# A four-layer kernel on one core: both mixtures norm turned rows inside their body and store per tile, and the decay attention norms in its projections and works in 64-token blocks

## The chip, the cores and the metric

The kernel runs on one core of one Trainium2 chip. The metric is the device time of one execution in microseconds (us); less is better. A core has TensorE (PE, with its weight loads shown apart as PEld), VectorE (DVE), ScalarE (ACT), GpSimd (POOL), and SyncE (SP), which here only issues DMAs. Engines run their own programs and wait for each other by semaphores. Everything is f32, so each matmul shows as two passes in the trace.

## The reference, cut to what matters

The input is 4 sequences of 1024 tokens with 128 features. A layer norm stands before each layer, and each layer adds to x:

```python
x = x + attn_a(_layernorm(x), ...)      # delta attention, 8 heads: untouched here
x = x + ffn(_layernorm(x), ...)         # first mixture, "f1"
x = x + attn_b(_layernorm(x), ...)      # decay attention
x = x + ffn(_layernorm(x), ...)         # second mixture, "f2", same weights

# ffn (mixture of 15 experts, 3 used per token, and a shared one)
shared = relu(xt @ sW1 + sb1) @ sW2 + sb2
probs = softmax(xt @ router_W + router_b)
top_p, top_i = top_k(probs, 3)          # cw: those three, zero elsewhere
h = relu(einsum('nd,edh->neh', xt, eW1) + eb1)
routed = einsum('ned,ne->nd', einsum('neh,ehd->ned', h, eW2) + eb2, cw)

# attn_b, per head of 64: a state that decays per feature
state = (1.0 - wt)[..., None] * state + kt[..., None] * vt[..., None, :]
out = einsum('bhd,bhde->bhe', rt, state)
```

## The kernel before

The 4096 tokens lie turned (features on partitions) in `g.xT`, their normed copy in `g.xn`; a tile is 512 tokens, NT = 8.

`build` calls the stages one after another: `delta_attention`, `normed_mixture` "f1", `decay_attention`, `normed_mixture` "f2", `store_rows`. Each is a block of its own with one hand-written program per engine; the order of lines in such a program is the order on that engine, and blocks are parted by a barrier.

`normed_mixture` has two parts. In the lead all eight tiles are normed on turned data (`centre`, `variance` and `replicate` on PE, `take` and `root` on ACT, `invert` and `norm` on DVE), with the router of tile 0 between them. In the body PE goes over tiles n and experts e: `hidden(n, e + 2)` makes a hidden tile into bank `ph`, ACT takes its relu into `hr`, DVE scales it by its gate into `hs`, and PE adds its product to `py`. Tile n's body also makes the router of tile n+1: `r_lt` and `r_tr` on PE, `r_sub`, `r_top`, `r_cwt` on DVE, `r_exp` on ACT. The gates go by SP to DRAM (`gates_d`) and come back spread over all partitions (`gates`, in four groups, double-buffered):

```python
for n in range(NT):
    sp.wait_ge(ct_ev, n + 1)
    sp.dma_start(gates_d[n % 2], cwt[n % 2][0:E_N, :]).then_inc(gates_out, 16)
```

`decay_attention` calls `layernorm`, a block of its own, then projects each tile (five products: z in two steps, k, r, v). `near(l, b)` makes, for level l and sequence b, the 32x32 blocks of a triangular product for levels 0 to 5, which DVE keeps by mask in `Pc`; `merge(l, b)` on DVE then doubles the span of the decays; levels 6 and 7 are `far`, kept by ACT in `P`, where ACT also lays `Pc` down (`spread`). `steps()` gives the order: levels 0 and 1 of a sequence stand behind the tiles that complete it. A scan over chunks ends the stage. `store_rows` turns the result back and stores it in four DMAs.

Of the kernel before, what the change touches and what calls it, by code (L numbers as in the profile page):

```python
# [42 lines left out]
def constants():  # L43
# [14 lines left out]
    s, t = a[:, None] % 32, np.arange(32)[None, :]  # L58
    bm = [(s == t).astype(np.float32)]
    for l in range(5):  # L60
        h = 1 << l
        bm.append(((s // (2 * h) == t // (2 * h)) & (s // h < t // h)).astype(np.float32))
# [19 lines left out]


def store_rows(nc, g):

    with ExitStack() as ctx:  # L86
        new_sem = semaphores(nc, ctx)
        xo = ctx.enter_context(nc.sbuf_tensor("xout", [128, NTOK // 128, D], F32))
        ps = [ctx.enter_context(nc.psum_tensor(f"st{i}", [128, TILE], F32)) for i in range(4)]
        turned, kept, stored = (new_sem(n) for n in ("st_turned", "st_kept", "st_stored"))  # L90
        block = ctx.enter_context(nc.Block())
        dst = g.dram["out"].rearrange("b t d -> (b t) d").rearrange("(j p) d -> p j d", p=128)

        @block.tensor
        def _(pe):
            for i in range(NT):
                if i >= 4:
                    pe.wait_ge(kept, i - 3)
                for a in range(4):
                    o = TILE * (i % 2) + 128 * a  # L100
                    last = nc.tensor.transpose(ps[i % 4][:, 128 * a:128 * a + 128], g.xT[:, i // 2, o:o + 128], g.ident[:, :])  # L101
                last.then_inc(turned, 1)

        @block.scalar
        def _(act):
            for i in range(NT):
                act.wait_ge(turned, i + 1)
                nc.scalar.activation(xo[:, 4 * i:4 * i + 4, :], ps[i % 4][:, :].rearrange("p (a d) -> p a d", a=4), ACT.Copy).then_inc(kept, 1)  # L108

        @block.sync  # L110
        def _(sp):
            for q in range(4):
                sp.wait_ge(kept, 2 * q + 2)
                sp.dma_start(dst[:, 8 * q:8 * q + 8, :], xo[:, 8 * q:8 * q + 8, :]).then_inc(stored, 16)
            sp.wait_ge(stored, 64)


def layernorm(nc, g, tag, src, affine=None, fetch=None, fetched=None):

    QUARTER = TILE // 4  # L120
    EPS = 1e-5
    root_scale, root_bias = (1.0, EPS) if affine is None else (1.0 + EPS, EPS * EPS)
    with ExitStack() as ctx:
        new_sem = semaphores(nc, ctx)
        sb = lambda n, s: ctx.enter_context(nc.sbuf_tensor(tag + n, s, F32))
        pb = lambda n: [ctx.enter_context(nc.psum_tensor(f"{tag}{n}{i}", [128, TILE], F32)) for i in range(2)]
        cen, var, rep = pb("cen"), pb("var"), pb("rep")
        xc = sb("xc", [128, 4, TILE])
        sq = sb("sq", [128, 2, TILE])
        rs = sb("rs", [128, 4, QUARTER])  # L130
        eps = sb("eps", [128, 1])
        centred, squared, copied, varied, rooted, inverted, spread, scaled, normed, eps_ready = (
            new_sem(tag + n) for n in ("centred", "squared", "copied", "varied", "rooted", "inverted", "spread", "scaled", "normed", "eps_ready"))
        block = ctx.enter_context(nc.Block())

        if fetch is not None:
            @block.sync
            def _(sp):
                fetch(sp)

        @block.tensor
        def _(pe):
            def centre(i):
                if i >= 2:
                    pe.wait_ge(copied, i - 1)
                nc.tensor.matmul(cen[i % 2][:, :], g.centre[:, :], src(i), start=True, stop=True).then_inc(centred, 1)

            def variance(i):
                pe.wait_ge(squared, i + 1)
                if i >= 2:  # L150
                    pe.wait_ge(rooted, i - 1)
                for q in range(4):
                    last = nc.tensor.matmul(var[i % 2][32 * q:32 * q + 32, 0:QUARTER], g.mean[:, 0:32], sq[:, i % 2, QUARTER * q:QUARTER * (q + 1)], start=True, stop=True)
                last.then_inc(varied, 1)

            def replicate(i):
                pe.wait_ge(inverted, i + 1)
                if i >= 2:
                    pe.wait_ge(scaled, i - 1)
                for q in range(4):  # L160
                    last = nc.tensor.matmul(rep[i % 2][:, QUARTER * q:QUARTER * (q + 1)], g.pick[:, q, :], rs[:, i % 4, :], start=True, stop=True)
                last.then_inc(spread, 1)
            centre(0)
# [1210 lines left out]
def normed_mixture(nc, g, tag):  # L1374
# [5 lines left out]
    with ExitStack() as ctx:  # L1380
# [62 lines left out]
        def _(pe):  # L1443
# [52 lines left out]
            for i in range(NT + 1):  # L1496
# [6 lines left out]
                if i == 2:  # L1503
                    r_lt(0)
# [528 lines left out]
```

## Time and profile before

| | us |
|---|---|
| three runs | 3269.03, 3266.42, 3254.58 (median 3266.42) |
| profiled execution: its own time | 3265.66 |
| its span in the trace | 3263.9 |
| PE busy | 3048.2 (93%) |
| DVE busy | 2505.7 (77%) |
| ACT busy | 2268.4 (70%) |
| POOL busy | 1947.9 (60%) |

The span is what the trace shows from first to last instruction. Shares are averages over stages with different limits, so what a stage waits for is read in that stage. A row of the timeline gives start, duration, engine, line, operation, output and inputs, shape and count, and in brackets how long the engine sat idle before it and what ended that; a count joins neighbouring instructions of one line.

### The profile page before, as it was taken

How to read it: one execution, taken by the hardware profiler on the slowest of the kernel's cores; microseconds unless marked ns; L12 is line 12 of the kernel's file. 1: busy time of each engine (PE TensorE's matmuls, PEld its weight loads, DVE VectorE, ACT ScalarE, POOL GpSimd, SP SyncE). 2: the span in 40 equal slices, each digit the busy share in tenths (PEclk: the TensorE clock that was granted, in tenths of full speed). 3: DMA queues.
4: the chain of work that ended last, by engine and by line, in shares of the span. 5: the costliest groups of instructions: out<-in, count | busy, mean ns of one | idle time of the engine just before them, and what ended most of it. 6: DMA issues, size and time to landing. Idle time of an engine off the chain costs nothing. (4 is left out here: it accounts for less than half of the span.)

```text
span 3263.9 us, 86845 instructions
## 1 busy us (share of the span) xinstructions
PE 3048.2 (93%) x29020; PEld 2370.3 (73%) x29020; DVE 2505.7 (77%) x5782; ACT 2268.4 (70%) x6848; POOL 1947.9 (60%) x3091
## 2 busy tenths in 40 slices
PE   5569999999999999999999999999998999848998
PEld 3448888888888888888888888888774444545444
DVE  5669999999999999999999999999654443664443
ACT  4768888888888888888888888888543333323333
POOL 1588888888888888888888888888710000000000
PEclk8779999999999999999999999999998999959999
DMA  4456776767777767777677767767432322002323
GB/s 100 122 146 169 190 187 170 178 170 179 182 185 178 173 177 178 174 184 182 176 176 175 179 172 187 183 168 177 122 95 84 137 106 103 5 4 76 146 98 123
DMA packets 587924, 482.94 MB, mean 148 GB/s; under 512 B 464492, under 2 KB 504076, under 8 KB 581340
## 3 DMA queue, kind: packets, MB, share of 16 engines
q1 hardware_dynamic: 587484, 477.39, 55.1%
q8 instruction: 237, 3.88, 0.5%
q14 instruction: 203, 1.66, 0.2%
HBM read 285.39 MB, written 191.86 MB: 146 GB/s over the span
## 5 line engine op out<-in xcount | busy, mean ns | idle before, releaser
L1058 DVE SCALAR_TENSOR_TENSOR conv_k<-PP,tk,conv_k 128x256 f32<-128x256 f32 x1536 | 722.6, 479 | 61.0 <-ACT conv_k L893 33.5
L831 POOL TENSOR_TENSOR X<-X,tmp 96x31 f32<-96x31 f32 (+15 forms) x992 | 534.5, 539 | 77.8
L1058 DVE SCALAR_TENSOR_TENSOR conv_v<-PP,tv,conv_v 128x256 f32<-128x256 f32 x1152 | 539.0, 477 | 45.0 <-ACT conv_v L893 35.4
L828 POOL TENSOR_TENSOR tmp<-At,X 96x31 f32<-96x31 f32 (+15 forms) x992 | 486.3, 490 | 63.2 <-DMA At<-n_d 5.0
L1227 PE MATMUL PP<-xn,wk 128*128 128x268 f32 x1024 | 342.2, 418 | 35.9 <-DVE conv_k L1058 27.9
L814 POOL TENSOR_TENSOR rk<-ss,half 96x8 f32<-96x8 f32 x128 | 209.1, 1633 | 175.1 <-DVE ss L1026 175.1
L796 POOL TENSOR_TENSOR Sg<-S,gend 128x512 f32<-128x512 f32 x256 | 266.0, 1039 | 62.0 <-DVE S L1017 62.0
L865 ACT ACTIVATE recA<-TG,es 96x128 f32<-96x128 f32 x1024 | 285.1, 369 | 5.3 <-DVE es L1051 5.3
L893 ACT ACTIVATE conv_k<-PP,tk 128x256 f32<-128x256 f32 x512 | 245.4, 481 | 54.9 <-PE PP L1227 47.6
L1191 PE MATMUL RB<-rhs,Yf 96*96 96x128 f32 x2048 | 269.0, 274 | 14.6 <-DVE rhs L1006 14.5
L857 ACT ACTIVATE recA<-TG 128x128 f32<-128x128 f32 x1024 | 265.5, 272 | 24.6 <-PE TG L1278 24.6
L883 ACT ACTIVATE ws<-RB 96x512 f32<-96x512 f32 x256 | 151.7, 592 | 184.0 <-PE RB L1191 181.1
L1181 PE MATMUL RA<-S,kqgB 128*96 128x128 f32 x2048 | 276.2, 278 | 1.0 <-DVE S L1017 1.0
L1201 PE MATMUL RA<-ws,recB 96*128 96x128 f32 x2048 | 271.6, 275 | 0.2 <-ACT ws L883 0.2
L1191 PEld LDWEIGHTS RB<-rhs,Yf 96*96 96x96 f32 x2048 | 242.2, 163 | 37.0 <-DVE rhs L1006 24.6
L1201 PEld LDWEIGHTS RA<-ws,recB 96*128 96x128 f32 x2048 | 259.9, 192 | 8.1 <-ACT ws L883 0.8
L1290 PE MATMUL TG<-kq 128*96 128x128 f32 x1888 | 245.2, 273 | 1.2 <-ACT recA L865 1.0
L1181 PEld LDWEIGHTS RA<-S,kqgB 128*96 128x96 f32 x2048 | 233.4, 163 | 13.0 <-DVE S L1017 4.4
L781 POOL TENSOR_TENSOR kqgA<-kq,gdec 128x768 f32<-128x768 f32 x128 | 203.2, 1587 | 38.4 <-ACT kq L934 31.6
L1290 PEld LDWEIGHTS TG<-kq 128*96 128x96 f32 x1888 | 219.0, 163 | 2.2 <-ACT recA L865 2.2
L1227 PE MATMUL PP<-xn,wv 128*128 128x268 f32 x768 | 218.5, 391 | 1.2 <-DVE conv_k L1058 1.2
L1227 PEld LDWEIGHTS PP<-xn,wk 128*128 128x128 f32 x1024 | 161.5, 197 | 67.2 <-issue 34.2
(280 smaller groups left out, 6751.2 us busy)
## 6 DMA issues: line engine op xcount, KB each, us to landing
kqg_d<-kqgA SPq DMA_DIRECT2D x128, 512.0 KB, 6.3
kqgB<-kqg_d SPq DMA_DIRECT2D x128, 512.0 KB, 4.4
rec_d<-recA SPq DMA_DIRECT2D x128, 480.0 KB, 3.4
recB<-rec_d SPq DMA_DIRECT2D x128, 480.0 KB, 5.8
f1gates<-f1gates_d SPq DMA_DIRECT2D x24, 1024.0 KB, 6.8
f2gates<-f2gates_d SPq DMA_DIRECT2D x24, 1024.0 KB, 6.8
gdec<-gdec_d SPq DMA_DIRECT2D x128, 128.0 KB, 5.6
apk_d<-apkA SPq DMA_DIRECT2D x128, 128.0 KB, 3.3
```

The source lines that it names most:

```text
L796: nc.gpsimd.tensor_tensor(Sg[:, :, :], S[cc][:, :, :], d.broadcast_to([128, B, 128]), ALU.mult).then_inc(sg_ev[cc], 1)
L828: nc.gpsimd.tensor_tensor(t, At[q % 2][:, j, j + 1:].unsqueeze(2).broadcast_to(sh), X[q % 2][:, j, 0:cols].unsqueeze(1).broadcast_to(sh), ...
L831: nc.gpsimd.tensor_tensor(x, x, t, ALU.subtract).then_inc(sub_ev, 1)
L857: last = nc.scalar.activation(recA[N % 2][:, u * 128:(u + 1) * 128], TG[:, u, :], ACT.Square, accum_out=ksum[:, u:u + 1])
L865: last = nc.scalar.activation(recA[N % 2][0:R, u * 128:(u + 1) * 128], TG[0:R, u, :], ACT.Copy, scale=es[:, u, TC - 1:TC])
L893: nc.scalar.activation(acc, src[:, :, 0:SPAN], ACT.Copy, scale=w).then_inc(tap0_ev[i], 1)
L1058: return nc.vector.scalar_tensor_tensor(acc, src[:, :, j:j + SPAN], w[:, j:j + 1], acc, ALU.mult, ALU.add)
L1181: last = mm(RA[0:R, b, :], kqgB[N % 2][:, b * NCC + cc, 0:R], S[cc][:, b, :], start=True, stop=True)
L1191: last = mm(RB[0:R, b, :], Yf[N % 2][:, b * NCC + cc, :], rhs[:, b, :], start=True, stop=True)
L1201: last = mm(RA[:, b, :], recB[N % 2][:, u * 128:(u + 1) * 128], ws[cc][:, b, :], start=True, stop=True)
L1227: mm(out, w, x, start=True, stop=True).then_inc(tile_mm[i], 1)
L1290: last = mm(gram_bank(N, hf)[0:R, u % HU, :], kq[N % 2][:, u, 0:R], kq[N % 2][:, u, :], start=True, stop=True)
```

## The change

In both mixtures the norm goes into the body. PE turns a tile back to rows (`rows_of`), DVE centres it (`centre`), ACT squares it with a sum per token (`square`), GpSimd raises variance to -1/2, DVE scales (`norm`), PE turns it again (`hat`), ACT keeps it in `g.xn` (`keep_xn`). Tiles 0 and 1 pass ahead of the body; tile n+2 passes inside tile n. The router's logits come as rows from one set of four matmuls (`r_lg`), and DVE adds the bias. `ph` has three banks. The second mixture stores by tile: `store_turn` on PE, `keep_out` on ACT, `out_rows` on SP; `store_rows` and `layernorm` are gone. In the decay attention the same norm stands in the projections, two tiles ahead, with one bank each for the two turns; the block width W is 64, levels 0 to 6 are near, only 7 is far, and `P` is cleared in eight pieces.

```diff
 @block.sync                                  # normed_mixture
+        def out_rows(sp, n):
+            sp.wait_ge(st_ev, n + 1)
+            dst = d["out"].rearrange("b t d -> (b t) d")[TILE * n:TILE * (n + 1), :].rearrange("(a p) d -> p a d", p=128)
+            sp.dma_start(dst, xo[:, n % 2, :, :]).then_inc(stored[n % 2], 16)
...
                     sp.dma_start(gates[n % 2][:, a:b, :], gates_d[n % 2, a:b].partition_broadcast(128)).then_inc(gates_in[n % 2][k], 16)
+                if last and n:
+                    out_rows(sp, n - 1)
...
 @block.tensor
+            rows_of(0)
+            rows_of(1)
+            hat(0)
+            r_lg(0)
+            hat(1)
...
+                    if e == 1:
+                        rows_of(n + 2)
+                    if e == 11:
+                        hat(n + 2)
                     if n + 1 < NT:
                         if e == 0:
-                            r_lt(n + 1)
-                        if e == 2:
-                            r_tr(n + 1)
+                            r_lg(n + 1)
                         if e == 7:
                             r_ct(n + 1)
+                    if last and n and e == 14:
+                        store_turn(n - 1)
+            if last:
+                store_turn(NT - 1)
...
 @block.scalar
+            def keep_out(n):
+                act.wait_ge(st_mm, n + 1)
+                if n >= 2:
+                    act.wait_ge(stored[n % 2], 16 * (n // 2))
+                nc.scalar.activation(xo[:, n % 2, :, :], turn_bank(0), ACT.Copy).then_inc(st_ev, 1)
...
+                    if e == 6:
+                        square(n + 2)
+                    if e == 13:
+                        keep_xn(n + 2)
+                    if last and n and e == 15:
+                        keep_out(n - 1)
...
 @block.gpsimd
+                nc.gpsimd.tensor_tensor(rs[:, n % 2, :], var[:, n % 2, :], mhalf[:, :], ALU.pow).then_inc(rs_ev, 1)
...
 @block.vector
+                    if e == 4:
+                        centre(n + 2)
+                    if e == 7:
+                        var_eps(n + 2)
+                    if e == 10:
+                        norm(n + 2)
                     if n + 1 < NT:
-                        if e == 3:
+                        if e == 2:
                             r_sub(n + 1)
...
 def decay_attention(nc, g):
-    MASKED = 6
+    MASKED, W = 7, 64
...
-        pair_of = lambda n: 2 + n % 2 if n < 2 * B else n % 4
+        pair_of = lambda n: 3 if n < 2 * B else n % 4
...
             def tile(i):                     # PE
+                rows_of(i + 2)
+                pe.wait_ge(xn_ev, i + 1)
...
+                hat(i + 1)
...
             def tile(i):                     # DVE
+                var_eps(i + 1)
+                centre(i + 2)
+                norm(i + 1)
...
-                        for c in range(4):
-                            t0 = (b * NGB + q) * 128 + 32 * c
-                            o = pair[pair_of(n)][32 * c:32 * c + 32, h, 32 * q:32 * q + 32]
+                        for c in range(0, 128, W):
+                            t0 = (b * NGB + q) * 128 + c
+                            o = pair[pair_of(n)][c:c + W, h, W * q:W * q + W]
```

SP's program in the second mixture, before, from the gates of tile 1 on (`f2cwt` the gates as made, `f2gates_d` in DRAM, `f2gates` spread):

```order
L1436 DMA f2gates_d<-f2cwt 15x512
L1440 DMA f2gates<-f2gates_d 128x2048 x3
L1440 DMA f2gates<-f2gates_d 128x1536
L1436 DMA f2gates_d<-f2cwt 15x512
L1440 DMA f2gates<-f2gates_d 128x2048 x3
L1440 DMA f2gates<-f2gates_d 128x1536
```

The same place in the change, as far as the gates of tile 3:

```order
L1302 DMA f2gates_d<-f2cwt 15x512
L1306 DMA f2gates<-f2gates_d 128x2048 x3
L1306 DMA f2gates<-f2gates_d 128x1536
L1286 DMA out_dram<-f2xo 128x4x128
L1302 DMA f2gates_d<-f2cwt 15x512
L1306 DMA f2gates<-f2gates_d 128x2048 x3
L1306 DMA f2gates<-f2gates_d 128x1536
L1286 DMA out_dram<-f2xo 128x4x128
L1302 DMA f2gates_d<-f2cwt 15x512
```

Between the gates of a tile and those of the next now stands a store of 512 tokens, for whose rows SP waits.

PE's program of the second mixture, before, around the start of tile 2 (the row with `f2cwt` opens a tile; `f2ph` are hidden tiles, `f2py` the sums):

```order
L1523 MATMUL f2py<-f2hs,f2w 128x512
L1492 MATMUL f2ph<-xn,f2w 128x512
L1523 MATMUL f2py<-f2hs,f2w 128x512
L1492 MATMUL f2ph<-xn,f2w 128x512
L1523 MATMUL f2py<-f2hs,f2w 128x512
L1519 MATMUL f2py<-f2cwt,f2b 128x512
L1492 MATMUL f2ph<-xn,f2w 128x512
L1523 MATMUL f2py<-f2hs,f2w 128x512
L1469 MATMUL f2pl<-xn,f2rw 16x512
```

The same place in the change:

```order
L1388 MATMUL f2py<-f2hs,f2w 128x512
L1369 MATMUL f2ph<-xn,f2w 128x512
L1388 MATMUL f2py<-f2hs,f2w 128x512
L1349 MATMUL f2pr<-ident,xT 128x128 x4
L1369 MATMUL f2ph<-xn,f2w 128x512
L1388 MATMUL f2py<-f2hs,f2w 128x512
L1384 MATMUL f2py<-f2cwt,f2b 128x512
L1369 MATMUL f2ph<-xn,f2w 128x512
L1388 MATMUL f2py<-f2hs,f2w 128x512
L1341 MATMUL f2pt<-f2rw,xn 128x15 x4
L1369 MATMUL f2ph<-xn,f2w 128x512
```

The turns of the tile to be stored stand behind the product of expert 14, and the logits of the next tile come from four matmuls of 15 columns.

PE's program of the decay attention, before, tile 2 and the first near block (`b_z` is the first step of z, `b_V`'s product has `b_w` as input):

```order
L1757 MATMUL b_pair<-xn,b_w 128x512
L1759 MATMUL b_pair<-xn,b_w 128x512
L1761 MATMUL b_pair<-xn,b_w 128x512
L1763 MATMUL b_pair<-b_z,b_w 128x512
L1766 MATMUL b_pair<-b_w,xn 128x128 x4
L1796 MATMUL b_pair<-b_rF,b_kB 32x32 x64
```

The same place in the change:

```order
L1675 MATMUL b_pair<-ident,xT 128x128 x4
L1692 MATMUL b_pair<-xn,b_w 128x512
L1694 MATMUL b_pair<-xn,b_w 128x512
L1696 MATMUL b_pair<-xn,b_w 128x512
L1684 MATMUL b_pair<-ident,b_rows 128x128 x4
L1699 MATMUL b_pair<-b_z,b_w 128x512
L1702 MATMUL b_pair<-b_w,xn 128x128 x4
L1732 MATMUL b_pair<-b_rF,b_kB 64x64 x32
```

The turn of tile 4 stands ahead of the products and that of tile 3's normed rows between them, and the block's 64 matmuls of 32x32 are now 32 of 64x64.

## Rows read from the trace of the kernel before

**Rows 1.** Stages: length, busy us (instructions) of each engine, granted clock, DMA.
```profile
core 0: us, PE busy (x) PEld busy (x) DVE busy (x) ACT busy (x) POOL busy (x), PEclk, DMA share, GB/s
2480.00:2518.90 38.90, 33.11 (x166) 17.10 (x167) 16.58 (x45) 17.21 (x31) 0.00 (x0) 0.76 0.34 101
2518.90:2768.60 249.70, 247.63 (x619) 105.81 (x618) 109.57 (x289) 94.36 (x141) 0.00 (x0) 0.99 0.30 120
2768.60:2836.10 67.50, 63.09 (x912) 37.91 (x912) 38.03 (x56) 28.91 (x50) 6.93 (x1) 0.97 0.04 11
2836.10:2928.30 92.20, 39.56 (x2817) 36.64 (x2817) 64.13 (x99) 18.48 (x28) 0.00 (x0) 0.56 0.02 4
...
2967.40:3004.40 37.00, 29.61 (x166) 16.59 (x166) 16.68 (x45) 17.79 (x32) 0.00 (x0) 0.86 0.37 107
```

**Rows 2.** Timeline of the second mixture's first gates; last, a stage as in rows 1.
```profile
2997.22 0.32 SPq L1436 DMA_DIRECT2D f2gates_d<-f2cwt  x1
2998.74 2.03 SPq L1440 DMA_DIRECT2D f2gates<-f2gates_d  x4
3003.70 1.89 DVE L1663 TENSOR_TENSOR f2hs<-f2gates,f2hr 128x512 f32<-128x512 f32 x3 [6.51 <-DMA f2gates<-f2gates_d]
3004.45 2.08 PE L1523 MATMUL f2py<-f2hs,f2w 128*128 128x512 f32 x2 [1.66 <-DVE f2hs L1663]
...
3006.00:3008.00 2.00, 2.00 (x3) 0.13 (x2) 0.00 (x0) 0.00 (x0) 0.00 (x0) 0.57 1.01 427
```

**Rows 3.** Timeline of the second mixture's body, a tile's boundary and router.
```profile
3011.66 1.06 PE L1475 MATMUL f2pt<-ident,f2lt 16*128 16x16 f32 x8
...
3033.80 1.02 PE L1492 MATMUL f2ph<-xn,f2w 128*128 128x512 f32 x2
3037.63 1.02 PE L1523 MATMUL f2py<-f2hs,f2w 128*128 128x512 f32 x2
3038.58 1.03 PE L1469 MATMUL f2pl<-xn,f2rw 128*16 128x512 f32 x2
3046.05 0.69 DVE L1663 TENSOR_TENSOR f2hs<-f2gates,f2hr 128x512 f32<-128x512 f32 x1 [0.70 <-ACT f2hr L1575]
3048.83 1.34 DVE L1663 TENSOR_TENSOR f2hs<-f2gates,f2hr 128x512 f32<-128x512 f32 x2
3054.20 0.34 SPq L1436 DMA_DIRECT2D f2gates_d<-f2cwt  x1
```

**Rows 4.** Timeline of the end, and the store's line: times of one, first and last start.
```profile
3251.74 0.69 DVE L1648 TENSOR_TENSOR xT<-f2py,xT 128x512 f32<-128x512 f32 x1 [1.43 <-PE f2py L1523]
3253.82 3.69 PE L101 MATMUL st<-ident,xT 128*128 128x128 f32 x32 [2.12 <-PEq L78]
3254.49 4.03 ACT L108 ACTIVATE xout<-st 128x512 f32<-128x512 f32 x8 [4.64 <-PE st L101]
...
L114 SPq DMA_DIRECT2D out_dram<-xout x4: 372/380/389, 3255.6 to 3258.5; - x4
```

**Rows 5.** Timeline of VectorE and GpSimd in the prologue, and of GpSimd later.
```profile
8.40 1.21 DVE L410 TENSOR_REDUCE p_nm<-p_xin 128x8 f32<-128x1024 f32 x1
11.32 2.48 POOL L401 TENSOR_TENSOR p_rs<-p_var,p_mhalf 128x8 f32<-128x8 f32 x1 [10.37 <-DVE p_var L422]
...
2350.47 0.70 POOL L807 TENSOR_TENSOR fo<-fo,minus_half 128x2 f32<-128x2 f32 x1
```

**Rows 6.** Timeline of the decay attention's levels, all engines.
```profile
2876.82 0.72 DVE L1930 COPY_PREDICATED b_Pc<-b_masks,b_pair 128x512 f32<-128x512 uint32 x1 [1.22 <-PE b_pair L1796]
2878.75 0.69 DVE L1947 TENSOR_TENSOR b_F<-b_F 128x512 f32<-128x512 f32 x1
2879.11 1.61 PE L1796 MATMUL b_pair<-b_rF,b_kB 64*32 64x32 f32 x128 [2.23 <-issue]
2880.67 0.72 DVE L1930 COPY_PREDICATED b_Pc<-b_masks,b_pair 128x512 f32<-128x512 uint32 x1 [1.23 <-PE b_pair L1796]
...
2924.47 3.75 ACT L1880 ACTIVATE b_P<-b_pair 64x1024 f32<-64x1024 f32 x4
```

More of the change, by code:

```diff
@@ L81, in semaphores @@
     return sem
[L84 to L115, printed above, removed]
@@ L1444, in _ @@
             mm = nc.tensor.matmul
-            def centre(i):
-                need(pe, copied, i - 2)
-                mm(cen[i % 2][:, :], g.centre[:, :], x_of(i), start=True, stop=True).then_inc(centred, 1)
-            def variance(i):
-                pe.wait_ge(squared, i + 1)
-                need(pe, rooted, i - 2)
-                for q in range(4):
-                    last = mm(var[i % 2][32 * q:32 * q + 32, 0:QUARTER], g.mean[:, 0:32], sq[:, i % 2, QUARTER * q:QUARTER * (q + 1)], start=True, stop=True)
-                last.then_inc(varied, 1)
@@ L1457, in replicate, with rows_of @@
-            def replicate(i):
-                pe.wait_ge(inverted, i + 1)
-                need(pe, scaled, i - 2)
-                for q in range(4):
-                    last = mm(rep[i % 2][:, QUARTER * q:QUARTER * (q + 1)], g.pick[:, q, :], rs[:, i % 4, :], start=True, stop=True)
-                last.then_inc(spread, 1)
-            def r_lt(n):
+            def rows_of(n):
+                if n >= NT:
+                    return
+                if n > 1:
+                    pe.wait_ge(xn_ev, n)
+                for a in range(4):
+                    end = nc.tensor.transpose(turn_bank(n)[:, a, :], x_of(n)[:, a * 128:(a + 1) * 128], g.ident[:, :])
+                end.then_inc(rows_mm, 1)
@@ L1465, in r_lt, with hat, r_lg @@
+            def hat(n):
+                if n >= NT:
+                    return
+                pe.wait_ge(hat_ev, n + 1)
+                for a in range(4):
+                    end = nc.tensor.transpose(turn_bank(n)[:, a, :], rows[:, n % 2, a, :], g.ident[:, :])
+                end.then_inc(hat_mm, 1)
+            def r_lg(n):
                 if n == 0:
                     pe.wait_ge(router_in, 32)
-                    pe.wait_ge(scaled, 1)
-                need(pe, ct_ev, n - 1)
-                mm(pl[0:NE, :], rw[:, :], xn_of(n), start=True, stop=True).then_inc(lt_mm, 1)
@@ L1863, in _, with square, keep_xn @@
         def _(act):
+            def square(i):
+                if i >= NT:
+                    return
+                act.wait_ge(cent_ev, i + 1)
+                need(act, sq_ev, i - 1)
+                for a in range(4):
+                    last = nc.scalar.activation(sq[:, a, :], rows[:, i % 2, a, :], ACT.Square, accum_out=var[:, i % 2, a:a + 1])
+                last.then_inc(sq_ev, 1)
+            def keep_xn(i):
+                if i >= NT:
+                    return
+                act.wait_ge(hat_mm, i + 1)
+                nc.scalar.activation(xn_of(i), bank[5], ACT.Identity, scale=gain[:, 0:1], bias=gain[:, 1:2]).then_inc(xn_ev, 1)
             def tile(i):
@@ L1892, in _ @@
                 tile(i)
-            act.wait_ge(cleared, 1)
-            for b in range(B):
-                far(MASKED, b)
+            act.wait_ge(cleared, NT)
             for b in range(B):
@@ L1949, in _ @@
             nc.vector.memset(S[:, 0, :, :], 0.0).then_inc(z_ev, 1)
+            centre(0)
+            centre(1)
+            var_eps(0)
+            norm(0)
             dve.wait_ge(loaded, 16 * len(loads))
@@ L2014, in build @@
         decay_attention(nc, g)
-        normed_mixture(nc, g, "f2")
-        store_rows(nc, g)
+        normed_mixture(nc, g, "f2", last=True)
 def kernel(**inputs):
```

404 lines of the change are left out of this document (191 added, 213 removed).

## The prediction

> **What bounds the kernel now.** I read the page's busy tenths first: TensorE is at nine tenths nearly throughout, so I cut the span into stages [rows 1] and read the chain inside each. The first 2480 us (delta attention) are untouched. Behind them each mixture has a lead, in which all eight tiles are normed and the first router and gates are made (38.9 and 37.0 us), and a body in which TensorE is busy 248 of 250 us. Between them stand the decay attention's norm and projections (67.5 us), its levels (92.2 us, TensorE busy 39.6, VectorE 64.1), and a scan that stays.
>
> What ends the waits: the lead ends when the gates have come back from DRAM; the first scaled tile waits 6.51 us for that DMA [rows 2]. In a body matmuls stand end to end: a pair of passes takes 1.02 us and overlaps the next [rows 3]. In the levels neither VectorE nor TensorE is full: each block waits 1.23 us for its matmuls, and TensorE sits 2.23 us with no releaser shown before 128 short matmuls [rows 6]. I read that as its instruction supply: 256 instructions (128 loads, 128 matmuls) per 3.85 us.
>
> **The mixture's lead.** Now it holds two tiles instead of eight. From the block's start at 2967.4 I add: four turns 0.5; VectorE centres tile 0, then tile 1, at 1.5 each (a 128x1024 sum takes 1.21 [rows 5]; at half the width 0.65 for the sum, 0.2 for a small scale, 0.65 for the add); variance, power and norm 0.15 + 1.2 + 0.7; turn back 1.0 at low clock; copy 0.7. The first normed tile stands 7.8 us in. Router matmuls 1.7 at low clock, bias, maximum and subtract 0.8, tile 1's copy, which ScalarE has ahead of the exponential, 0.8, table load and exponential 1.5, top three 2.2, turn 1.1, copy 0.7: 16.6 in. Then the road of before, from gates' write to first scaled tile: 2997.22 to 3003.70, 6.5 us [rows 2]. Sum 23.1; before it is 36.3 (2967.4 to 3003.70). **Gain 13.0** in the second mixture. The first starts with TensorE at half clock (0.76 granted over its lead against 0.86 [rows 1]): 24.2 against 38.1 before (its lead's 38.9 less 0.75), **13.9**. Weights land earlier than they are wanted, as VectorE no longer clears a tile ahead of their issue.
>
> The power on GpSimd is the uncertain piece. 128x2 takes 0.70 and 128x8 took 2.48 [rows 5]; I take 1.2 for 128x4, with those as bounds. The Trainium skill's page "GPSIMD Engine Reference", section 8, says GpSimd shares its SBUF interfaces with VectorE and suffers beside instructions with two SBUF inputs. That speaks for the upper bound, which by rows costs 1.3 us on each of three starts and 1 us on each of six decay tiles: 10 us in all.
>
> **The body.** Per tile on TensorE: out go the router's product and the turn of its result (1.03 and 1.06 [rows 3]); in come four matmuls with the tile as weights, eight passes, which I price as the eight passes of that turn, 1.06; and for six of eight tiles two sets of four turns, 0.46 each (32 turns in 3.69 us [rows 4]). That is even to 0.5 us per mixture. Three PSUM banks for hidden tiles instead of four cost nothing: hidden e+3 is issued behind product e, which itself needs relu e. VectorE's slack is thin. Scaled tile 6 starts 2.8 us behind tile 5 because of the top three [rows 3], and centring behind tile 4 now moves tile 5 by 0.4: tile 6 is ready 0.1 to 0.2 us late for its product, **1 us** per mixture. ScalarE's four squares and the copies delay one relu by less than its scaled tile has to spare.
>
> **The stores, where I see the largest term.** In the second mixture SP's program reads: gates of tile n, then the store of tile n-1, then gates of tile n+1. The store waits for its copy, and ScalarE makes that copy behind relu 15 of tile n. Before, gates of n+1 left SP at that tile's expert 8 (3054.20, some 15 us ahead of need); now they are queued behind that store. With the rows of the tile boundary [rows 3]: the instruction behind product 14 starts 3033.8, and there the store's turns are put in: with their waits to 3034.5; copy 0.6, to 3035.2; store issue 0.4; gates' write at 3035.6; 1.52 to the reads' issue [rows 2], and 0.5 for 256 KB queued ahead (0 to 1.5, one more such round), so 3037.6; 4.96 to the first scaled tile; 0.75 to its product: 3043.3. Without that wait this product starts 3037.63 + 0.65 for the store's turns = 3038.3. TensorE stands **5.0 us** (4.5 to 6). VectorE and ScalarE stop too, as buffers fill; nothing is left to do in advance.
>
> After the wait comes the clock. At 3004.45, after 1.7 us of nothing and a thin stretch, a pair of passes takes 2.08 instead of 1.02, and the clock granted up to 3008 is 0.57 [rows 2]: 3.6 us at 1.2 GHz cost 1.8. I add that to every stall, **6.8 each**. The Trainium skill's page "TensorE: Matmul & The Clock Gate", section "HAM oscillation", describes such waits as making every round start cold. [...] Rows decide for 1.8, with 0 and 6 (the first mixture's lead, where half clock holds far longer) as bounds. Gates of tiles 2 to 7 are behind a store: six stalls, **+41** (4.5 to 12 each: 27 to 72). Turns for seven stores in the body: 7 x 0.65 = **+4.5**.
>
> **The end.** Before, 12.2 us pass from the last add (3251.74) to the span's end, with the last store's issue at 3258.5 [rows 4]. Now: add 0.7, turns 0.6, copy 0.6, one store of 256 KB issued at +2.0, landing and close 3.6 (before: 5.4 for double the bytes): 5.6. **Gain 6.6**.
>
> **The decay attention.** Before: 159.7 us from 2768.6 to 2928.3 [rows 1]. Now, by VectorE: first normed tile at 9.8 (as above, with one turning bank and a clock at half); tiles 0 and 1 add 6.1 each, since the chain is variance, centre, norm (2.5), turn back 0.5, second product 0.95, V product 1.0, V's copy 0.7, and waits; 22.0. Tiles 2 to 7 add near blocks. With 64 tokens a block has 1024 elements a partition instead of 512; a copy of 512 takes 0.72, of which the next hides 0.1 [rows 6]; for 1024 I take the 1.21 of a 128x1024 row less that, 1.14 [rows 5]. Merges take 1.14 at level 0 and 1.92 above (block and merge of 512 span 2.62, 2876.82 to the end of its last, 2879.44, less copy and overlap [rows 6]). Cycles: 8.5 (level 0) or 9.2 (level 1); last two 8.3 and 6.7, having nothing left to norm: 50.4. So 72.4 to the merge of near(1,2). Then near(0,3) and near(1,3) one after the other in the one pair of banks, 6.5; twenty near blocks of levels 2 to 6 at 1.14 + 1.92 = 3.06, 61.2; level 7's four merges 7.7. Sum 147.8: **gain 11.9**. TensorE now needs 128 instructions a block, 1.93 us by the supply above, so VectorE is never kept waiting. ScalarE, which ended the stage before, is covered: its copies of 64x1024 take 0.94 (four in 3.75 [rows 6]), the last spread follows near(6,3) at 138.4, two of these and four of the last level end at 144.
>
> **The sum.** -13.9 + 0.5 + 1 (first mixture), -11.9, -13.0 + 0.5 + 1 + 4.5 + 41 - 6.6 (second) = +3.1, on the profiled execution's 3265.66: 3269. Its median of three is 3266.42, so nothing is to be corrected. A measurement here tells about 0.5%, 16 us, from no change.
>
> **Rivals.**
> - *Stalls last longer* (slower, 0.15): TensorE stays at 1.2 GHz well into each tile, as in the first mixture's lead, where 0.76 is granted. Cost 6 instead of 1.8, +25: 3294. It decides from 4.0 lost per stall on. For: after each stall work resumes one product at a time. Against: in the second mixture full clock was back at 3008 [rows 2].
> - *Stores hold nothing up* (faster, 0.10): then 41 fall away, 3228. For: gates are double-buffered. Against: SP takes its program in order, and its row for the next gates stands behind the store.
> - *64-token blocks bring nothing* (0.09): the wide copy costs 1.24 and tiles run 1 us longer each, by the slow power: decay +1, so 3282, on the edge of slower.
> - *Forecast* (0.66): 3269, itself between 3254 and 3284.
>
> Chances: faster 0.13 (no stalls, and a little of the forecast's lower end), same 0.65, slower 0.22 (long stalls, part of the third case). The range is 3250 to 3291: pow, clock and copy bounds, leaving out the two outer cases' ends.
>
> **What the next profile shows.** Right: six waits of VectorE in the second mixture for the gates' DMA, some 10 us each, none in the first; tile period 31.5 in the first mixture and 39 in the second; leads of 23 to 25 us; copies of 64-token blocks near 1.2 us with VectorE back to back in levels 2 to 6; a tail under 6 us. Wrong: a second mixture at 32 us a tile; products behind a stall at 2.1 us for more than 5 us; first-mixture tiles over 32 us, which would mean VectorE's bursts hold TensorE; decay tiles over 10 us, the power or single bank being dearer than worked out.

## The result, and the profile after

The changed kernel takes 3273.58 us (median of 14 runs, 3270.69 to 3278.93), the kernel before 3266.1 us in 14 runs: a ratio of 1.0032, 95% interval 1.0024 to 1.004. That is within half a per cent, as forecast, and 4.6 us above the predicted 3269.0. Inside, five of the seven stages below moved by more than the 4.6 us that the total is off.

The changed kernel's stages, cut at events that both kernels have: first scaled tile and last add of the first mixture, the turns of k, the decay attention's last add, first scaled tile and last add of the second mixture, end. Columns as in [rows 1].

```profile
2504.05:2749.48 245.43, 244.64 (x652) 112.16 (x652) 123.73 (x327) 96.74 (x186) 6.04 (x6) 0.98 0.31 123
2749.48:2905.24 155.76, 104.01 (x2113) 78.57 (x2113) 121.65 (x175) 44.17 (x109) 15.36 (x17) 0.73 0.03 6
2905.24:2942.67 37.43, 36.54 (x296) 28.02 (x296) 17.10 (x43) 9.55 (x16) 0.00 (x0) 0.95 0.01 2
2942.67:2967.66 24.99, 13.45 (x36) 6.57 (x36) 8.79 (x36) 7.24 (x23) 2.11 (x3) 0.57 0.51 143
2967.66:3269.31 301.65, 272.39 (x680) 126.40 (x680) 122.64 (x327) 99.61 (x193) 6.04 (x6) 0.89 0.27 106
3269.31:3275.30 5.99, 0.66 (x4) 0.42 (x4) 0.69 (x1) 0.60 (x1) 0.00 (x0) 0.88 0.28 88
```

Set against the same marks of the trace before, and against the prediction's terms, in us:

| stage | before | after | moved | predicted |
|---|---|---|---|---|
| start to first scaled tile, first mixture | 2518.15 | 2504.05 | -14.1 | -13.9 |
| first mixture's body | 248.42 | 245.43 | -3.0 | +1.5 |
| decay attention, to the turns of k | 161.75 | 155.76 | -6.0 | -11.9 |
| its scan | 37.54 | 37.43 | -0.1 | 0 |
| second mixture's lead | 37.84 | 24.99 | -12.9 | -13.0 |
| second mixture's body | 248.04 | 301.65 | +53.6 | +47.0 |
| end | 12.16 | 5.99 | -6.2 | -6.6 |
| sum | 3263.9 | 3275.3 | +11.4 | +3.1 |

These are two single executions. The profiled one of after took 3277.11 us, 3.5 above its median, so the medians differ by only 7.5. Of e9_filled_lead below, one of five executions, 3260.24 us, was in a slower state with a lower clock; its median of 3204.3 counts it (3203.6 without), its ratio does not.

The second mixture's largest row is a tile boundary. SP's queue, then VectorE, then TensorE there:

```profile
3072.46 0.39 SPq L1286 DMA_DIRECT2D out_dram<-f2xo  x1
3072.89 0.51 SPq L1302 DMA_DIRECT2D f2gates_d<-f2cwt  x1
3074.96 1.96 SPq L1306 DMA_DIRECT2D f2gates<-f2gates_d  x4
...
3079.83 1.29 DVE L1564 TENSOR_TENSOR f2hs<-f2gates,f2hr 128x512 f32<-128x512 f32 x2 [9.86 <-DMA f2gates<-f2gates_d]
...
3074.50 1.13 PE L1369 MATMUL f2ph<-xn,f2w 128*128 128x512 f32 x2
3080.58 2.07 PE L1388 MATMUL f2py<-f2hs,f2w 128*128 128x512 f32 x2 [4.95 <-DVE f2hs L1564]
3082.45 1.73 PE L1341 MATMUL f2pt<-f2rw,xn 128*128 128x15 f32 x8
3084.01 2.06 PE L1369 MATMUL f2ph<-xn,f2w 128*128 128x512 f32 x2
3085.86 1.91 PE L1388 MATMUL f2py<-f2hs,f2w 128*128 128x512 f32 x2
3089.83 1.02 PE L1388 MATMUL f2py<-f2hs,f2w 128*128 128x512 f32 x2
```

The next tile's gates leave 0.43 us behind the store. VectorE then waits 9.86 us and TensorE 4.95 us. The six waits of TensorE are 4.46, 4.95, 4.62, 4.41, 5.15 and 4.88 us. What stands behind a wait runs at 1.2 GHz: pairs of passes take 2.07 instead of 1.02. The windows behind this wait, and then the second five us behind the third wait and the sixth, columns as above:

```profile
3080.50:3088.00 7.50, 7.42 (x17) 4.22 (x18) 3.18 (x8) 0.83 (x2) 0.00 (x0) 0.50 0.69 291
3088.00:3090.00 2.00, 2.00 (x6) 1.24 (x6) 0.00 (x0) 0.00 (x0) 0.00 (x0) 0.62 0.00 0
3090.00:3100.00 10.00, 10.00 (x27) 4.46 (x27) 6.74 (x29) 5.17 (x14) 1.01 (x1) 1.00 0.00 0
...
3126.21:3131.21 5.00, 5.00 (x11) 2.43 (x10) 0.69 (x1) 1.21 (x3) 0.00 (x0) 0.57 0.05 20
...
3245.87:3250.87 5.00, 5.00 (x12) 2.24 (x11) 1.61 (x3) 1.40 (x3) 0.00 (x0) 0.93 0.03 11
```

The clock is back 8.9 us after this wait. After the six waits in order it takes some 9.0, 8.9, 9.3, 6.2, 7.4 and 5.7 us, 7.7 in the mean, worked out from the granted clock of such windows; the order doesn't follow the length of the waits. After the short wait of before it took 3.6 [rows 2], and from that I had priced it. The line on all of VectorE's waits for gates in this stretch (in total, times, longest) holds the six and the first tile's:

```profile
DVE f2hs L1564 <- DMA f2gates<-f2gates_d: 64.3, 7, 10.1
```

In the first mixture a tile takes 30.93 us (gates' writes are issued at 2586.18, 2617.11, 2648.04). TensorE in one tile: the router's eight passes step on by 0.81 us, a set of four turns by 0.43.

```profile
2602.42 0.96 PE L1341 MATMUL f1pt<-f1rw,xn 128*128 128x15 f32 x8
2603.23 1.10 PE L1369 MATMUL f1ph<-xn,f1w 128*128 128x512 f32 x2
2604.17 1.02 PE L1388 MATMUL f1py<-f1hs,f1w 128*128 128x512 f32 x2
2605.03 0.60 PE L1324 MATMUL f1pr<-ident,xT 128*128 128x128 f32 x4
2605.46 1.02 PE L1369 MATMUL f1ph<-xn,f1w 128*128 128x512 f32 x2
```

GpSimd's power in the first mixture's body, with VectorE's multiply beside it, and then the decay attention: the power there, VectorE's wait for V in two tiles, two neighbouring blocks of the levels, and the turns of k.

```profile
2582.69 1.01 POOL L1463 TENSOR_TENSOR f1rs<-f1var,f1mhalf 128x4 f32<-128x4 f32 x1 [29.93 <-DVE f1var L1485]
2583.18 0.69 DVE L1564 TENSOR_TENSOR f1hs<-f1gates,f1hr 128x512 f32<-128x512 f32 x1 [0.58 <-ACT f1hr L1443]
...
2757.42 1.01 POOL L1873 TENSOR_TENSOR b_rs<-b_var,b_mhalf 128x4 f32<-128x4 f32 x1 [5.74 <-DVE b_var L1896]
...
2788.04 0.69 DVE L1911 COPY b_V<-b_pair 128x512 f32<-128x512 f32 x1 [1.90 <-PE b_pair L1702]
2798.00 0.69 DVE L1911 COPY b_V<-b_pair 128x512 f32<-128x512 f32 x1 [2.79 <-PE b_pair L1702]
...
2834.29 1.35 DVE L1923 COPY_PREDICATED b_Pc<-b_masks,b_pair 128x1024 f32<-128x1024 uint32 x1
2835.53 0.68 DVE L1937 TENSOR_TENSOR b_kB<-b_kB,b_F 128x512 f32<-128x512 f32 x1
2837.45 1.35 DVE L1923 COPY_PREDICATED b_Pc<-b_masks,b_pair 128x1024 f32<-128x1024 uint32 x1
2905.24 6.32 PE L1766 MATMUL b_pair<-ident,b_kB 128*128 128x128 f32 x32 [5.75 <-DVE b_F L1940]
```

A block now takes 3.16 us on VectorE, without a wait (before, one in 3.85 with 1.23 of waiting [rows 6]). The power takes 1.01 with VectorE idle beside it (2757.42) and with a multiply of two SBUF operands beside half of it (2582.69).

### The profile page after: what moved, and what is told of

It reads as the page before. It is cut to its first block and busy times, and to the rows that moved or that the text cites. A ratio compares the mean times of both kernels' runs of the same rounds, so it can differ in the third digit from the quotient of the medians.

```text
span 3275.3 us, 83441 instructions
## 1 busy us (share of the span) xinstructions
PE 3032.8 (93%) x27212; PEld 2378.3 (73%) x27212; DVE 2536.4 (77%) x5859; ACT 2249.8 (69%) x6953; POOL 1972.7 (60%) x3125
## 5 line engine op out<-in xcount | busy, mean ns | idle before, releaser
L1443 ACT ACTIVATE f2hr<-f2ph,f2b 128x512 f32<-128x512 f32 x128 | 87.1, 686 | 191.3 <-PE f2ph L1369 191.3
```

## The experiments

All runs were timed beside the kernel before on the same chip, whose medians there were 3266.4 to 3266.8. Stages that the verdicts rest on, from each profile, by the marks above; each is one execution, and the decay stage of one code moves by 3.4 us (new) and 4.5 us (old) from one to the next:

| kernel | first body | decay | second lead | second body | end | median |
|---|---|---|---|---|---|---|
| before | 248.42 | 161.75 | 37.84 | 248.04 | 12.16 | 3266.1 |
| after | 245.43 | 155.76 | 24.99 | 301.65 | 5.99 | 3273.6 |
| e1_gates_first | 245.68 | 152.51 | 24.13 | 249.26 | 5.9 | 3220.8 |
| e2_filled_stall | 245.73 | 152.43 | 24.08 | 279.82 | 5.96 | 3249.8 |
| e4_store_at_end | 245.73 | 152.32 | 24.02 | 244.63 | 12.17 | 3223.0 |
| e8_ready_store_ahead | 245.44 | 155.72 | 24.55 | 249.03 | 5.94 | 3223.6 |
| e3_old_decay | 245.74 | 166.24 | 24.57 | 303.47 | 5.96 | 3284.8 |
| e5_blocks_of_32 | 245.91 | 157.88 | 24.51 | 299.81 | 5.91 | 3276.7 |
| e6_order | 246.12 | 146.19 | 24.21 | 303.62 | 5.97 | 3268.6 |
| e7_both | 245.68 | 147.57 | 24.5 | 247.99 | 5.96 | 3213.3 |
| e9_filled_lead | 241.58 | 146.82 | 22.67 | 244.82 | 5.91 | 3204.3 |
| e10_order_again | 241.57 | 144.13 | 22.58 | 244.9 | 5.94 | 3201.0 |

**Gates ahead of the store.** Is SP's program order the cause of the stalls?

```diff
                     sp.dma_start(gates[n % 2][:, a:b, :], gates_d[n % 2, a:b].partition_broadcast(128)).then_inc(gates_in[n % 2][k], 16)
-                if last and n:
-                    out_rows(sp, n - 1)
+                if last and n > 1:
+                    out_rows(sp, n - 2)
             if last:
+                out_rows(sp, NT - 2)
                 out_rows(sp, NT - 1)
```

> The changed kernel, with SP's store of tile n-1 put behind the gates of tile n+1 instead of ahead of them. Read from the trace of after: the second mixture takes 301.65 us from its first scaled tile to its last add, the first takes 245.43; 7 x 0.44 of the 56.2 between them are the stores' turns, so 53.1 us are six stalls, 8.85 each (4.41 to 5.15 of waiting, the rest at half clock). Theory 1 (SP's program order is the whole cause): all of it goes, 3273.6 - 53 = 3220 us, no wait of VectorE for the gates but the first, tile period 31.4 as in the first mixture plus the turns. By the prediction's own stall of 6.8 it would be 3233. Rival (the stall comes from elsewhere in the boundary, as the one turning bank or ScalarE's copy of the output): it stays, 3265 to 3274.

Measured: 3220.8 us, ratio 0.9858 (0.9843 to 0.9873). SP's queue in its trace:

```profile
3022.10 0.34 SPq L1302 DMA_DIRECT2D f2gates_d<-f2cwt  x1
3023.65 1.78 SPq L1306 DMA_DIRECT2D f2gates<-f2gates_d  x4
3034.92 0.39 SPq L1286 DMA_DIRECT2D out_dram<-f2xo  x1
3053.47 0.34 SPq L1302 DMA_DIRECT2D f2gates_d<-f2cwt  x1
```

The reads of the gates leave 11.3 us ahead of the store instead of behind it, and VectorE waits for gates at the first tile alone. The second body falls from 301.65 to 249.26: the six stalls cost 52.4 us, 8.7 each (by the same pair of orders in e6_order and e7_both, 55.6 and 9.3). This meets the first theory's 3220 and rules out its rival.

**Work in place of the stall.** How much of the 8.7 is waiting, how much the clock?

```diff
                     hidden(n, e + 2)
+                    if last and n > 1 and e == 0:
+                        for _ in range(5):
+                            mm(pl[:, :], w1[:, 0, :], xn_of(n), start=True, stop=True)
                     pe.wait_ge(hs_ev[e], n + 1)
```

> The changed kernel, with ten more matmul passes (five pairs of 128x512) put on TensorE where it stands in each of the six stalls; their result is read by nobody. Five pairs take 4.3 us at full clock, the shortest wait is 4.41, so the wait stays as long and only the idle time goes. Theory 1 (of 8.85 us a stall, 4.75 are waiting and 4.1 are work at half clock behind it, which comes from the idle time): 3273.6 - 6 x 4.1 = 3249 us, and the product behind the wait takes 1.02 instead of 2.07. By the prediction's 1.8 us it would be 3263. Rival (the half clock comes from something else, or the 4.1 are waits of another kind): 3273, or slower by the matmuls that don't fit.

Measured: 3249.8 us, ratio 0.9947 (0.9934 to 0.9959). TensorE in its trace; L1389 are the added matmuls, L1391 the product:

```profile
3066.61 4.45 PE L1389 MATMUL f2pl<-xn,f2w 128*128 128x512 f32 x10
3071.71 1.13 PE L1391 MATMUL f2py<-f2hs,f2w 128*128 128x512 f32 x2 [0.65 <-DVE f2hs L1567]
3072.67 0.96 PE L1341 MATMUL f2pt<-f2rw,xn 128*128 128x15 f32 x8
```

The product is no earlier, but it and what follows run at 2.4 GHz, and the time meets the first theory's 3249. The body takes 279.82: the clock was worth 21.8 us (3.6 a stall), the wait 30.6 (5.1 a stall). By after's own rows the waits are 4.7 in the mean, which leaves 4.0 for the clock, so this split is known to some 0.4 us. The prediction's 1.8 was half of it.

**Stores at the end.** Does the norm in the body delay the gates? The store's turns, copies and DMAs leave the mixture, and `store_rows` of before comes back:

```diff
-        normed_mixture(nc, g, "f2", last=True)
+        normed_mixture(nc, g, "f2")
+        store_rows(nc, g)
```

> The changed kernel with its stores as before: no turns and no stores in the second mixture, all rows turned and stored behind it. Theory 1: the stalls go (-53), the seven sets of turns go (-3), the end grows back from 6.0 to 12.2 us behind the last add (+6): 3224 us, some 4 slower than the kernel with the gates ahead of the store. Rival (the new norm in the body is what makes the gates late): the second mixture keeps waits for its gates, and the time stays over 3265.

Measured: 3223.0 us, ratio 0.9863 (0.985 to 0.9877). Without stores the second body takes 244.63, so seven sets of turns cost 4.6 us (249.26 less 244.63; 3.4 by e7_both's body, which has the same program) and the norm in the body gains 3.4 (248.04 before). The end is 12.17 again. Stores in the body are worth 6.2 - 4.6 = 1.6 us when they hold nothing up, which the times (2.2 apart, with overlapping intervals) don't contradict.

**A ready store ahead of the gates.** Is it the waiting, or the 256 KB? Ahead of the gates of tile n now stands the store of tile n-3, where the changed kernel has that of n-2: one tile earlier, not two as the expectation says. SP's order is that of e1_gates_first, but the store now goes out right ahead of the gates.

```diff
                 sp.wait_ge(ct_ev, n + 1)
+                if last and n > 2:
+                    out_rows(sp, n - 3)
                 sp.dma_start(gates_d[n % 2], cwt[n % 2][0:E_N, :]).then_inc(gates_out, 16)
...
-                if last and n:
-                    out_rows(sp, n - 1)
             if last:
-                out_rows(sp, NT - 1)
+                for n in range(NT - 3, NT):
+                    out_rows(sp, n)
```

> The changed kernel, with a store still right ahead of each tile's gates on SP's queue, but that of a tile earlier by two, whose rows have long been copied when SP comes to it. It tells waiting from traffic. Theory 1 (the store's wait for its copy holds SP): no stalls, as with the gates first, 3220 to 3222 us. Rival (256 KB of output in the DMA queues ahead of the gates make them late): the gates are later by what these bytes take, 0.4 to 1.5 us, and if that were the cause the stalls of 8.85 stay, 3265 to 3274. If only the end costs more, as three stores are left there, 3222 to 3226.

Measured: 3223.6 us, ratio 0.9868 (0.9854 to 0.9881). SP's queue:

```profile
3053.83 0.39 SPq L1286 DMA_DIRECT2D out_dram<-f2xo  x1
3054.26 0.51 SPq L1304 DMA_DIRECT2D f2gates_d<-f2cwt  x1
3056.35 1.94 SPq L1308 DMA_DIRECT2D f2gates<-f2gates_d  x4
```

With the store's bytes ahead, the reads follow the gates' write by 2.09 us, without them by 1.55 (3022.10 to 3023.65 above): 0.54 us for the traffic, as the prediction's 0.5. It is hidden here, and there is no stall: VectorE waits for gates at the first tile alone. The waiting is the cause. The time is 2.8 us above e1_gates_first, but the end is no longer (5.94 against 5.9); in the trace the decay stage has 3.2 of it, whose code is the same.

**The decay attention as before.** What are its norm in the projections and its 64-token blocks worth together? The function of before replaces the new one, with the 32-token masks.

> The changed kernel with the decay attention as before: its norm ahead of the projections, 32-token blocks. By the trace of after, from the stage's start to the turns of k it now takes 153.6 us (2751.6 to 2905.24) against 159.7: undoing it costs 6.1, 3279.7 us. By the prediction's 11.9 it would cost 11.9, 3285.5. Rival (the stages trade, as the first mixture's end and the clock at the stage's start are others now): another number than the window's, within 3 us of 3273.6.

Measured: 3284.8 us, ratio 1.0056 (1.0044 to 1.0069). Undoing it costs 11.2 us by the medians, close to the 11.9 of the prediction, and 7.8 by the ratios (1.0056 against 1.0032). That is above the 6.0 that two single traces gave. The stage itself differs between executions of one code: the new one has 155.76 and 155.72 in two traces, 152.3 to 152.5 in three; the old one 161.75 and 166.24. In all five traces the new stage starts with some 10 to 14 us at half clock. After and e8_ready_store_ahead meet half clock again in two of their tiles, e1_gates_first in none: from one copy of V to the next these two tiles take 9.96 and 10.3 us, against 9.06 and 8.74. e2_filled_stall and e4_store_at_end have one tile of 10.6, but a start that is 1.7 shorter. In after half clock comes up in the midst of a tile, and these rows take 1.92 and 1.82 where others of the same line take 1.05 and 1.16.

```profile
2786.95 1.05 PE L1702 MATMUL b_pair<-b_w,xn 128*128 128x128 f32 x8
2787.93 1.16 PE L1732 MATMUL b_pair<-b_rF,b_kB 64*64 64x64 f32 x64
...
2794.67 0.66 PE L1684 MATMUL b_pair<-ident,b_rows 128*128 128x128 f32 x4 [2.41 <-DVE b_rows L1902]
2796.04 1.92 PE L1702 MATMUL b_pair<-b_w,xn 128*128 128x128 f32 x8
2797.89 1.82 PE L1732 MATMUL b_pair<-b_rF,b_kB 64*64 64x64 f32 x64
```

The means of the traces (153.7 of five, 164.0 of two) differ by 10.3. Why some executions lose the clock there and others don't stays open.

**Blocks of 32 with the new norm.**

```diff
...
-    s, t = a[:, None] % 64, np.arange(64)[None, :]
+    s, t = a[:, None] % 32, np.arange(32)[None, :]
...
-    MASKED, W = 7, 64
+    MASKED, W = 6, 32
...
             act.wait_ge(cleared, NT)
+            for b in range(B):
+                far(MASKED, b)
```

> The changed kernel with 32-token blocks in the decay attention, and its norm still in the projections; level 6 goes back to the far blocks. It splits the 6 us in two. In levels 2 to 5 of before, a block took 3.85 us on TensorE's supply of 256 instructions; of after, 3.15 on VectorE, with four more blocks. Sixteen blocks of levels 2 to 5 at 3.85 and four of level 6 far, against twenty at 3.15: 61.6 + some 8 against 63.0, so blocks of 64 would be worth 6 to 7 us and the norm in the projections about nothing. Under the tile loop the 256 instructions of each of the eight near blocks there take 2 us more of TensorE than 128, and VectorE a third less per block. Theory 1: 3279 to 3284 us. Rival (64-token blocks bring nothing, the norm brought the 6): 3272 to 3275.

Measured: 3276.7 us, ratio 1.0032 (1.0021 to 1.0044): 3.1 us over after by the medians, none by the ratios. Neither theory met it. Its trace shows two effects against each other. From the ninth near block on, levels of 32-token blocks take 78.6 us (80.8 before), those of 64 take 71.0: some 8 us gained. VectorE waits there for TensorE, which stands before each block with no releaser shown:

```profile
2841.24 1.60 PE L1732 MATMUL b_pair<-b_rF,b_kB 64*32 64x32 f32 x127 [1.74 <-issue]
2844.83 1.61 PE L1732 MATMUL b_pair<-b_rF,b_kB 64*32 64x32 f32 x128 [1.99 <-issue]
```

I read that as its supply of instructions. The granted clock is 0.54 over this stretch, and no run tells the two apart.

Ahead of the ninth block, where VectorE also norms and copies, blocks of 32 take 79.2 us against 81.6 (e1_gates_first) to 84.8 (after). Blocks of 64 give 2.4 to 5.6 of the 8 back there, where the 1024-wide copy and mask lie on VectorE, which also norms. Net they are worth 0 to 3 us by the times (2.1 to 5.6 by the stage in single traces), the norm in the projections some 8 (3284.8 against 3276.7).

**Another order in the decay attention's tiles.** VectorE, TensorE and ScalarE in turn:

```diff
             def tile(i):
-                var_eps(i + 1)
-                centre(i + 2)
-                norm(i + 1)
                 dve.wait_ge(k_mm, i + 1)
                 nc.vector.tensor_copy(kB[:, TILE * i:TILE * (i + 1)], bank[1]).then_inc(k_ev, 1)
+                norm(i + 1)
+                centre(i + 2)
                 dve.wait_ge(v_mm, i + 1)
...
+            var_eps(1)
             norm(0)
...
                 if kind == "tile":
+                    if x:
+                        var_eps(x + 1)
                     tile(x)
...
-                hat(i + 1)
                 pe.wait_ge(zx_ev, i + 1)
                 mm(bank[0], w[:, 1, :], z1[:, i % 2, :], start=True, stop=True).then_inc(z_mm, 1)
+                hat(i + 1)
...
-                keep_xn(i + 1)
                 act.wait_ge(z_mm, i + 1)
                 nc.scalar.activation(F[:, TILE * i:TILE * (i + 1)], bank[0], ACT.Sigmoid, scale=-1.0, bias=neg_bw[:, :]).then_inc(f_ev, 1)
+                keep_xn(i + 1)
```

> The changed kernel with another order inside the decay attention's tiles, and nothing else: VectorE norms tile i+1 and centres tile i+2 between k's copy and V's copy of tile i, instead of ahead of k's copy, the variance's small operation goes to the end of the tile ahead, TensorE turns the normed rows back behind the second product, ScalarE makes F's sigmoid ahead of the normed copy. After's trace shows VectorE idle 1.9 to 3.5 us per tile for V's product, which stands on TensorE behind the turn that waits for the norm. Theory 1 (these waits are the order's, a serial chain of norm, turn back, second product, V): cycles of tiles 2 to 7 fall from 8.2 and 9.1 to some 6.7, 12 us in all, 3261 to 3265. Rival (each wait is made anew somewhere else, by ScalarE or TensorE): within 3 us of 3273.6.

> The changed kernel with the gates ahead of the store on SP and with the other order in the decay attention's tiles. The two lie in different stages, so their gains should add: 3220 - 10 = 3208 to 3212 us. If one eats the other's gain the sum falls short by more than 2 us.

Measured: 3268.6 us, ratio 1.0005 (0.9996 to 1.0013), 5.0 us under after by the medians, 8.8 by the ratios; with the gates first 3213.3, ratio 0.9834 (0.9821 to 0.9848), 7.5 and 7.8 under e1_gates_first. So some 7 us, and the two edits add. Less came of it than expected: e6_order met neither of its theories and e7_both is 1.3 above its range. Cycles fell from 8.2 and 9.1 to 7.0 and 7.9, not to 6.7. Three of VectorE's rows in a tile of e6_order:

```profile
2799.29 0.69 DVE L1906 COPY b_kB<-b_pair 128x512 f32<-128x512 f32 x1
2800.51 0.69 DVE L1902 TENSOR_TENSOR b_rows<-b_rows,b_rs 128x512 f32<-128x512 f32 x1 [0.53 <-POOL b_rs L1873]
2802.84 0.69 DVE L1910 COPY b_V<-b_pair 128x512 f32<-128x512 f32 x1
```

The wait for V is gone. In its place the norm waits 0.53 for the power, which the centring had covered.

**Filled leads.** The matmuls that nobody reads stand in the mixtures' leads too, added to e7_both:

```diff
+            def fill(k, bank):
+                for _ in range(k):
+                    mm(bank[:, :], g.ident[:, :], x_of(0), start=True, stop=True)
+
             rows_of(0)
             rows_of(1)
+            fill(5 if last else 2, pl)
             hat(0)
...
             hidden(0, 1)
+            fill(3 if last else 2, pl)
             r_ct(0)
...
                     hidden(n, e + 2)
+                    if n == 0 and e == 0:
+                        pe.wait_ge(bias_ev, 1)
+                        fill(4, pt)
```

> The kernel with the gates first and the other order in the decay attention's tiles (e7_both, 3213.3), and with matmuls that nobody reads put where TensorE stands in the two mixtures' leads: ahead of the first turn back, ahead of the gates' turn and ahead of the first product (5, 3 and 4 pairs of passes in the second mixture, 2, 2 and 4 in the first). In after's trace the second mixture's lead has TensorE at 0.59 of its clock, and from the first product (2968.41) to the third (2977.43) pass 9.0 us, against 4.8 at full clock. Theory 1 (half clock follows the idle time in the leads as in the stalls): 4.2 us of the body and some 2 of the lead's matmuls come back in the second mixture, and the 4.2 or less in the first, where the lead begins at half clock: 3213 - 6 to 10 = 3203 to 3207. Rival (a start like this stays cold, and the added matmuls at half clock take 1.71 a pair and come out late): 3213 to 3220.

Measured: 3204.3 us, ratio 0.9809 (0.9794 to 0.9824), 9.0 us under e7_both by the medians, 8.2 by the ratios. The first product in the second mixture, and the third:

```profile
2946.12 5.13 PE L1374 MATMUL f2pt<-xT,ident 128*128 128x512 f32 x8
2951.09 1.02 PE L1398 MATMUL f2py<-f2hs,f2w 128*128 128x512 f32 x2
...
2955.86 1.02 PE L1398 MATMUL f2py<-f2hs,f2w 128*128 128x512 f32 x2
```

4.8 us from one to the other, where after needs 9.0. Each body is 3 to 4 us shorter, the second lead 1.8. The first theory's 3203 to 3207 holds.

**The order again,** against the kernel before this one, with V's product ahead of the turn back, and the variance's small operation ahead of the merge:

```diff
-                hat(i + 1)
                 need(pe, v_ev, i - 1)
...
                 last.then_inc(v_mm, 1)
+                hat(i + 1)
...
-                    if x:
-                        var_eps(x + 1)
                     tile(x)
+                    if x < 2:
+                        var_eps(x + 2)
...
                     near(*x)
+                    if x[0] < 2 and 2 * x[1] + x[0] + 4 < NT:
+                        var_eps(2 * x[1] + x[0] + 4)
                     merge(*x)
```

> The kernel before this one (filled leads), with two more steps of order in the decay attention's tiles: V's product goes ahead of the turn back of the next tile's rows, and the variance's small operation goes ahead of the merge. In the trace of the other order (e6_order) VectorE waits 0.53 for the power and 0.2 for V per tile, up to 1.6 where TensorE waits for the norm, in cycles of 7.0 and 7.9; its own work is 5.5 and 6.3. Theory 1: cycles of 6.5 to 7, 3 to 5 us less than the kernel before this one. Rival (the stage now waits for ScalarE's chain of copies and sigmoids): within 2 us of it.

Measured: 3201.0 us, ratio 0.9802 (0.9789 to 0.9815). The stage takes 144.13 us, against 146.19 to 147.57 in the three traces of the order before it. The medians are 3.3 apart, the ratios 2.3, and their intervals overlap, so a gain in the total is likely but not shown, and neither the theory nor its rival is met. It has the lowest median: 66 us under before, 73 under the changed kernel.

## Why the prediction was right, and where not

- **The stores' stall** was right in place, cause and count: six stalls, gates queued on SP behind a store that waits for its copy (e1_gates_first, e8_ready_store_ahead). Waiting was priced 5.0 and measures 5.1 by e2_filled_stall, 4.7 by after's rows.
- **The clock behind the stall** was mis-sized: 1.8 in the sum, 3.6 by e2_filled_stall (4.0 by the other split), 11 to 13 us over six stalls. The step that failed took the 3.6 us at 1.2 GHz after a wait of 1.7 us [rows 2] for what follows a wait of 5 us; here it lasts 5.7 to 9.3. That the longer wait is why is not tested. The bounds were 0 and 6; no run shows the 0. The rival with long stalls put its turning point at 4.0, so it was missed narrowly, and its sign did show: products at 2.07 and 1.91 us for more than 5 us. The Trainium skill's page "TensorE: Matmul & The Clock Gate", section "HAM oscillation", says that rounds with such waits start cold each time. By that rule the trace agrees: behind every one of the six the granted clock is 0.50.
- **The leads** were right to 0.2 us (-14.1 and -12.9 against -13.9 and -13.0). The terms listed up to the first normed tile add to 7.25 and stand summed as 7.8, which is what the trace shows. The power, priced 1.2 between 0.70 and 2.48 [rows 5], took 1.01. The Trainium skill's "GPSIMD Engine Reference", section 8, warns of contention with VectorE instructions that have two SBUF inputs; here the power takes 1.01 with a multiply of that kind beside half of it and without one, so this case shows none.
- **The body** was priced at a cost of 0.5 us and 1 us of VectorE's bursts, +1.5. It gained 3.0 and 3.4. Two things failed. The sum was wrong: by its own prices 7 x 2.09 go out and 7 x 1.06 and 12 x 0.46 come in, a gain of 1.7 and not a cost of 0.5. And I gave four matmuls with the tile as weights the 1.06 of the old turn [rows 3]; they step on by 0.81, and a set of turns by 0.43. By steps from one start to the next (for what goes out 0.96, 3038.58 to 3039.54, and 0.99, 3011.66 to 3012.65, in the trace before) the gain is 2.8. The bursts cost nothing that shows: TensorE is busy 244.64 of 245.43 us.
- **The store's turns** were priced 4.5 us and cost 4.6 (e1_gates_first against e4_store_at_end) or 3.4 (e7_both against it). **The end** was priced at a gain of 6.6 and gave 6.2.
- **The decay attention** was priced at 11.9. Undoing it measures 11.2 by medians and 7.8 by ratios. The terms, in the one trace of after: 23.2 to the end of tile 1 (22.0 predicted), 52.3 for tiles 2 to 7 (50.4), 7.2 for the two blocks behind them (6.5), 63.0 for twenty blocks (61.2), 7.9 for level 7 (7.7). So the sum came out 5.8 short there. 1.8 of that is the wide predicated copy, 1.24 us to the next row instead of 1.14: the third rival's value for it was the right one. The 3.3 by which after's stage exceeds the shorter traces lie in its tiles at half clock and come in some executions alone. One tile there took 10.3 us, a sign that I had named as wrong; what its rows show is half clock and not the dear power named for it, which took 1.01.
- **The other signs** mostly showed: six waits of VectorE of 9.4 to 10.1 us for gates and none in the first mixture's tiles, 30.93 us a tile there for the 31.5 given, 39.1 to 41.0 in the stalled tiles for 39, and a tail of 5.99.

The forecast was right in where the time goes, and its small error in the total was luck: +11 for the clock and some +1 to +4 for the decay attention stand against -9 for the two bodies.

## What to carry to other kernels

A queue that takes its program in order passes a wait on to all that stands behind it. Before a store or load is put on it, compare when its data are ready with when the next transfer on that queue is due, and issue in the order of readiness; here two moved lines were worth 53 us. A wait of 4.4 to 5.2 us on TensorE cost here three quarters as much again at half clock: price it by rows behind waits of the same length, and where it can't be removed, matmuls that nobody reads can take that part back. The wider block shortened the levels by 8 us and lengthened the tiles, where VectorE also norms, by 2.4 to 5.6: weigh a wider tile stage by stage.

## What the runs showed of the hardware

- Behind a wait of 4.4 to 5.2 us TensorE's granted clock was 0.50 for 5.7 to 9.3 us of unbroken matmuls (after); with matmuls in the wait (0.65 us of it left) it stayed at 1.00, 2.4 GHz (e2_filled_stall).
- The decay stage, the same code in five kernels, was granted half clock at different places and took 152.3 to 155.8 us; over one stretch of 5 us the clock was 0.70 in after (2794 to 2799) and 1.00 at about the same place of e1_gates_first (2801 to 2806).
- The predicated copy of 128x1024 took 1.29 to 1.35 us, against 1.22 to 1.23 for a masked multiply of the same shape (24 and 4 rows of after).
- On one queue, a 256 KB store ahead of a small write delayed the reads behind it by 0.54 us (2.09 in e8_ready_store_ahead, 1.55 in e1_gates_first).
